# Second attention of a two-layer gated cross-attention kernel: the order of VectorE's work in a step

## The chip, the cores and the metric

The kernel runs on one core of a Trainium2 chip. The metric is the time of one execution on the device in microseconds, median of several runs. Times within a profile are microseconds from the first instruction of the core.

## The reference, cut to what matters

Sixty-four sequences of 128 tokens with 128 features go through two layers, each a gated cross-attention on a context of 77 tokens and a gated feed-forward part. The first feed-forward is a mixture of 16 experts, the second a matrix in FP8 rounding. The change lies in the third pass of the kernel, which finishes the first feed-forward (it gathers the experts' results), and does the second layer:

```
x = x + tanh(g_ffn[0]) * L0_ffn(_layernorm(x))            # its gather and sum are in the third pass
x = x + tanh(g_xattn[1]) * L1_xattn(_layernorm(x), ctx)   # 16 heads of 8, softmax over 77 keys
x = x + tanh(g_ffn[1]) * L1_ffn(_layernorm(x))            # quantize, 128 x 128 matmul, bias
_layernorm(x) = (x - mean(x)) / sqrt(var(x) + 1e-5)
```

## The kernel before, in words

All engines run their own program and meet at semaphores. The kernel has three passes: the first attention and routing (to about 480 us), the experts (to about 700 us), and the second layer, `step_c`. This last pass is a software pipeline: step t works on item t - lag for each operation, with 64 items and 81 steps; `t.at(lag)` gives the item or None where the pipeline fills or drains. The steps are written out one by one. Within a step each engine executes its operations in the order written; a wait at one of them holds everything behind it on that engine. `wait_edge` is a wait that is only emitted for steps below 18 and from 64 on; for the steps between, the order of the others implies it.

The operations that the text speaks of, by line:

- VectorE: L1073 and L1095 add the two gathered expert results to the residual (lag 1). L1078 and L1156 prepare the rounding. L1083 normalises the residual for the attention (`xn3`, lag 2); it needs GpSimd's reciprocal root L637 of the step before. L1065 takes the maxima of the scores in two halves (`largest`, lag 5). L1090 normalises for the last feed-forward (`xb4`, lag 9). L1100 adds the attention's result (lag 8); before it stands a wait for the key projection KT of this step. L1108 writes the masked keys. L1117 and L1122 take statistics (lags 8 and 1), L1131 and L1136 aggregate them to mean and variance, L1151 adds epsilon to both variances. L1126 is the reciprocal of the denominators (lag 7), L1141 multiplies the numerators by it (`OT1`), L1161 makes the output.
- GpSimd: L603 (a part of the rounding), L607 (adds a bias to the residual), L595 twice (the indirect gathers of this step's item), L615, L620, L622, L626 (rounding), and last L637, the power -0.5 of both variances, which waits for L1151.
- TensorE: the projections and transposes at the front of a step; then, behind a wait for the product L1141 of the step before, the scores (8 matmul records) and their transposed form ST (48 records) in one run; Y1 and KT (2 records each); mxT, the transpose of the maxima (1 record), behind the wait for both maxima; then the values V1, the denominators and the numerators (24 records each, line L1172 with 128*32 tiles).
- ScalarE: its first operation in a step, L656 twice, waits for ST; L744 is the exponential.

`par` picks one of two buffers. The variances and reciprocal roots have two, so that step t reads what step t - 1 wrote.

Of the kernel before, what the change touches and what calls it, by code (L numbers as in the profile page):

```python
# [7 lines left out]
ALU = mybir.AluOpType  # L8
ACT = mybir.ActivationFunctionType
X = mybir.AxisListType.X  # L10
P = 128
# [41 lines left out]
def wait_free(engine, sem, value):  # L53

    if isinstance(value, int) and value <= 0:
        return
    engine.wait_ge(sem, value)  # L57
# [24 lines left out]
def wait_edge(engine, t, sem, value):  # L82


    if t.edge:
        wait_free(engine, sem, value)


def flamingo_two_layers(nc, a, out, xs_dram, ys_dram):
# [37 lines left out]
    with ctx:  # L127
# [3 lines left out]
        def sem(name):  # L131
            return ctx.enter_context(nc.semaphore(name))
# [49 lines left out]
        PS = ctx.enter_context(nc.psum_tensor("PS", [P, 8, 512], F32))  # L182
# [82 lines left out]
        rd1 = cc(P)  # L265
        OT1 = cc(P)
# [32 lines left out]
        s = {n: sem(n) for n in names}  # L299
# [477 lines left out]
        def _(dve):  # L777
            V = nc.vector
# [8 lines left out]
            def res(b):  # L787
                return XR[:, bass.ds(b, 1), :].rearrange("q o d -> q (o d)")
# [269 lines left out]
            def step_c(t):  # L1058

                def largest(i):  # L1060

                    if (b := t.at(5)) is not None:
                        dve.wait_ge(s["S1_mm"], b + 1)
                        wait_edge(dve, t, s["mxT_mm"], b)
                        V.tensor_reduce(mx1[:, 2 * i * KEYS:2 * (i + 1) * KEYS].rearrange("q (g k) -> q g k", g=2)[:, :, 0:GH],  # L1065
                                        PS[:, 2 * i:2 * i + 2, 0:GH * J].rearrange("q g (h j) -> q g h j", j=J), X,
                                        ALU.max).then_inc(s["mx1_made"], 1)
# [6 lines left out]
                if (b := t.at(11)) is not None:  # L1074
                    p = t.par(11)
                    dve.wait_ge(s["z4_made"], b + 1)
                    wait_free(dve, s["q4_made"], b - 1)
                    V.tensor_scalar(c4[p].bitcast(I32), z4[t.ring(11, 4)].bitcast(I32), EXP_BITS, None,  # L1078
                                    ALU.bitwise_and).then_inc(s["m4_made"], 1)
                if (b := t.at(2)) is not None:  # L1080
                    dve.wait_ge(s["rsc_made"], b + 1)
                    wait_free(dve, s["xT3_mm"], b - 1)
                    V.tensor_scalar(xn3[t.par(2)], res(b), mvc[t.par(1)][:, 0:1], rsc[t.par(1)][:, 0:1], ALU.subtract,  # L1083
                                    ALU.mult).then_inc(s["xn3_made"], 1)
                largest(0)
                largest(1)
                if (b := t.at(9)) is not None:
                    wait_edge(dve, t, s["rsc_made"], b + 8)
                    wait_free(dve, s["z4_made"], b - 1)
# [28 lines left out]
                if (b := t.at(1)) is not None:  # L1118
# [1 line left out]
                    wait_edge(dve, t, s["agg3"], b)  # L1120
                    apart(dve)
                    V.bn_stats(st3, res(b)).then_inc(s["stats3"], 1)  # L1122
                if (b := t.at(7)) is not None:
                    dve.wait_ge(s["den_mm"], b + 1)
                    wait_free(dve, s["OT1_made"], b)
                    V.reciprocal(rd1, PS[:, 1, 0:P]).then_inc(s["rd1_made"], 1)  # L1126
                if (b := t.at(1)) is not None:
                    dve.wait_ge(s["stats3"], b + 1)
                    wait_free(dve, s["xn3_made"], b - 1)
# [2 lines left out]
                if (b := t.at(8)) is not None:  # L1132
# [1 line left out]
                    wait_free(dve, s["xb4_made"], b - 1)  # L1134
                    apart(dve)
                    V.bn_aggr(mvc[t.par(0)][:, 2:4], st4).then_inc(s["agg4"], 1)  # L1136
                if (b := t.at(7)) is not None:
                    dve.wait_ge(s["num_mm"], b + 1)
                    wait_free(dve, s["rd1_made"], b + 1)
                    wait_edge(dve, t, s["Y1_mm"], b)  # L1140
                    V.tensor_tensor(OT1, PS[:, 3, 0:P], rd1, ALU.mult).then_inc(s["OT1_made"], 1)  # L1141

                one, two = t.at(1), t.at(8)
                if one is not None or two is not None:
                    cols = slice(0 if one is not None else 1, 2 if two is not None else 1)
                    if one is not None:
                        dve.wait_ge(s["agg3"], one + 1)
                    if two is not None:
                        dve.wait_ge(s["agg4"], two + 1)
                    wait_edge(dve, t, s["rsc_made"], t.value - 2)  # L1150
                    V.tensor_tensor(vc[t.par(0)][:, cols], mvc[t.par(0)].rearrange("q (l c) -> q l c", c=2)[:, cols, 1],  # L1151
                                    epsc[:, cols], ALU.add).then_inc(s["varc_made"], 1)
                if (b := t.at(11)) is not None:
                    p = t.par(11)
                    dve.wait_ge(s["m4_made"], b + 1)
                    V.tensor_scalar(c4[p], c4[p], FP8_LEAST, FP8_ROUND, ALU.max, ALU.mult).then_inc(s["c4_made"], 1)  # L1156
# [6 lines left out]
            for span in c_spans():  # L1163
                run_steps(dve, NB, *span, step_c, TURN, LEADC)
# [288 lines left out]
```

## Time and profile before

| | |
|---|---|
| median of 3 runs | 1174.06 us (1169.97 to 1175.59) |
| the profiled execution's own time | 1175.44 us |
| its span | 1173.7 us |
| mean granted TensorE clock | 0.957 |
| busy: TensorE, its weight loads, VectorE, ScalarE, GpSimd | 88%, 72%, 70%, 50%, 55% |
| VectorE: L1065 | 128 times, mean 791 ns |
| VectorE: L1126 | 64 times, mean 954 ns |
| GpSimd: L595 (this pass) | 128 times, mean 1005 ns |

"PE" is TensorE's matmul row, "DVE" VectorE, "ACT" ScalarE, "POOL" GpSimd. In a timeline consecutive instructions of one line and kind are merged into one row (xcount), and the brackets give the idle time before the row and what released it. The granted clock is given as a share of 2.4 GHz.

### The profile page before, as it was taken

How to read it: one execution, taken by the hardware profiler on the slowest of the kernel's cores; microseconds unless marked ns; L12 is line 12 of the kernel's file. 1: busy time of each engine (PE TensorE's matmuls, PEld its weight loads, DVE VectorE, ACT ScalarE, POOL GpSimd, SP SyncE). 2: the span in 40 equal slices, each digit the busy share in tenths (PEclk: the TensorE clock that was granted, in tenths of full speed). 3: DMA queues.
4: the chain of work that ended last, by engine and by line, in shares of the span. 5: the costliest groups of instructions: out<-in, count | busy, mean ns of one | idle time of the engine just before them, and what ended most of it. 6: DMA issues, size and time to landing. Idle time of an engine off the chain costs nothing. (4 is left out here: it accounts for less than half of the span.)

```text
span 1173.7 us, 40437 instructions
## 1 busy us (share of the span) xinstructions
PE 1038.0 (88%) x13498; PEld 847.5 (72%) x13498; DVE 821.1 (70%) x2572; ACT 586.3 (50%) x1415; POOL 648.8 (55%) x1155
## 2 busy tenths in 40 slices
PE   4999999987999995699859996899999999998893
PEld 4788887865777774488758984677777777776672
DVE  1777777776777775655525555778888888887784
ACT  2666666653566662244425552345545545454464
POOL 2333333323777677567640005477777777777756
PEclk9999999997999997699979996999999999999997
DMA  3422113221443300244333331111111111111101
GB/s 74 88 49 46 38 45 75 72 68 45 106 105 89 90 19 29 84 137 145 107 92 112 109 91 48 32 30 37 44 40 43 44 40 43 43 41 41 39 24 31
DMA packets 106902, 74.39 MB, mean 63 GB/s; under 512 B 21360, under 2 KB 98288, under 8 KB 106736
## 3 DMA queue, kind: packets, MB, share of 16 engines
q1 hardware_dynamic: 98544, 55.40, 18.0%
q0 software_dynamic: 8192, 16.79, 4.7%
q8 instruction: 102, 1.67, 0.6%
q14 instruction: 64, 0.52, 0.2%
HBM read 38.60 MB, written 33.55 MB: 61 GB/s over the span
## 5 line engine op out<-in xcount | busy, mean ns | idle before, releaser
L656 ACT ACTIVATE arena<-PS 77x512 f32<-77x512 f32 (+4 forms) x736 | 304.9, 441 | 454.9 <-PE PS L1172 265.5
L1172 PE MATMUL PS<-arena 128*32 128x128 f32 (+5 forms) x9488 | 452.6, 291 | 49.9 <-issue 16.7
L1172 PEld LDWEIGHTS PS<-arena 128*32 128x32 f32 (+4 forms) x9488 | 352.0, 145 | 129.7 <-issue 37.1
L1172 PE MATMUL PS<-w,arena 128*128 x960 | 191.7, 318 | 1.2 <-ACT arena L656 0.4
L518 POOL DMA_INDIRECT moe_rows<-arena x128 | 127.4, 996 | 71.8 <-POOL arena L514 49.5
L533 POOL TENSOR_TENSOR arena<-arena,minus_half 128x2 f32<-128x2 f32 (+1 forms) x70 | 47.5, 679 | 188.3 <-DVE arena L830 166.6
L595 POOL DMA_INDIRECT arena<-moe_results,slot x128 | 128.7, 1005 | 40.7 <-issue 31.6
L1172 PEld LDWEIGHTS PS<-w,arena 128*128 128x128 f32 x960 | 135.5, 195 | 17.0 <-issue 4.5
L637 POOL TENSOR_TENSOR arena<-arena,minus_half 128x2 f32<-128x2 f32 (+1 forms) x71 | 51.1, 720 | 172.7 <-DVE arena L1151 168.9
L1053 DVE TENSOR_TENSOR arena<-PS,b_rows 128x256 f32<-128x256 f32 x160 | 67.8, 424 | 79.0 <-PE PS L1172 65.5
L1172 PEld LDWEIGHTS PS<-arena,wk_wq 128*128 128x128 f32 x512 | 80.6, 198 | 45.6 <-issue 43.0
L1172 PE MATMUL PS<-wo,arena 128*128 128x128 f32 x640 | 100.0, 288 | 2.2 <-ACT arena L656 1.4
L1172 PE MATMUL PS<-arena,wk_wq 128*128 128x154 f32 x512 | 98.3, 317 | 1.5 <-ACT arena L656 0.8
L1065 DVE TENSOR_REDUCE arena<-PS 128x8 f32<-128x616 f32 x128 | 96.0, 791 | 3.3 <-PE PS L1172 3.2
L719 ACT ACTIVATE arena<-PS 128x256 f32<-128x256 f32 x160 | 61.4, 384 | 72.7 <-PE PS L1304 66.9
L1172 PEld LDWEIGHTS PS<-wo,arena 128*128 128x128 f32 x640 | 83.9, 193 | 13.6 <-ACT arena L656 3.4
L744 ACT ACTIVATE arena<-PS 128x1536 f32<-128x1536 f32 x64 | 93.3, 1457 | 0.0
L540 POOL TENSOR_TENSOR arena<-arena 128x616 f32<-128x616 f32 x64 | 78.1, 1220 | 21.6 <-DVE arena L896 21.5
L867 DVE TENSOR_REDUCE arena<-PS 128x8 f32<-128x616 f32 x64 | 51.2, 800 | 54.2 <-PE PS L1172 54.2
L1046 DVE TENSOR_TENSOR arena<-PS,b_rows 128x128 f32<-128x128 f32 x160 | 46.1, 288 | 34.3 <-PE PS L1172 31.3
L1249 PE MATMUL PS<-ident,arena 128*77 128x128 f32 x512 | 68.8, 277 | 1.1 <-ACT arena L656 0.9
L1126 DVE RECIPROCAL arena<-PS 128x128 f32<-128x128 f32 x64 | 61.1, 954 | 12.3 <-PE PS L1172 8.8
(149 smaller groups left out, 1656.5 us busy)
## 6 DMA issues: line engine op xcount, KB each, us to landing
moe_rows<-zeros SPq DMA_DIRECT2D x64, 160.0 KB, 2.5
arena<-moe_rows SPq DMA_DIRECT2D x40, 256.0 KB
moe_results<-arena SPq DMA_DIRECT2D x40, 256.0 KB
residual<-in_x SPq DMA_DIRECT2D x64, 64.0 KB
w<-in_W SPq DMA_DIRECT2D x32, 128.0 KB
arena<-in_ctxC SPq DMA_DIRECT2D x64, 64.0 KB
out<-arena SPq DMA_DIRECT2D x64, 64.0 KB, 1.6
arena<-in_ctxT SPq DMA_DIRECT2D x32, 77.0 KB
```

Of the source, the lines that this page charges most:

```text
L518: g.indirect_dma_start(out=xs_flat[c][:, :], out_offset=bass.IndirectOffsetOnAxis(ap=si[2 * p + k], axis=0), in_=scat[p], in_offset=None). ...
L540: g.tensor_tensor(pv, pv, rd0[t.par(3)].rearrange("q (h o) -> q h o", o=1).to_broadcast([P, H0, J]), ALU.mult).then_inc(s["P0_made"], 1)
L595: g.indirect_dma_start(out=gy[k][p], out_offset=None, in_=ys_flat[c][:, :], in_offset=bass.IndirectOffsetOnAxis(ap=POS[k][:, b:b + 1], axi ...
L656: A.activation(o, i, ACT.Copy).then_inc(s[done], 1)
L719: A.activation(hT[p], PS[:, 4 + p, 0:EH], ACT.Relu).then_inc(s["hT_cp"], 1)
L744: A.activation(PT1[t.par(6)].rearrange("q (g w) -> q g w", g=NG), PS[:, 4:4 + NG, 0:TAIL], ACT.Exp, scale=DH1 ** -0.5).then_inc(s["exp1"], 1)
L867: V.tensor_reduce(mx0.rearrange("q (k h) -> q k h", k=2), sv, X, ALU.max).then_inc(s["mx0_made"], 1)
L1053: V.tensor_tensor(hb[p], PS[:, 2 + p, 0:EH], b1s[:, bass.ds(e, 1), :].rearrange("q o h -> q (o h)"), ALU.add).then_inc(s["h_made"], 1)
L1065: V.tensor_reduce(mx1[:, 2 * i * KEYS:2 * (i + 1) * KEYS].rearrange("q (g k) -> q g k", g=2)[:, :, 0:GH], PS[:, 2 * i:2 * i + 2, 0:GH * J] ...
L1126: V.reciprocal(rd1, PS[:, 1, 0:P]).then_inc(s["rd1_made"], 1)
L1172: return T.matmul(o, l, r, start=start, stop=stop)
L1249: last = T.transpose(PS[0:J, 2 + h // HB0, (h % HB0) * P:(h % HB0 + 1) * P], P0[p][:, h * J:(h + 1) * J], ident[:, :])
```

## The change

In VectorE's `step_c` the two calls of `largest` move ahead of the first normalisation (L1080 to L1084), and the reciprocal and the product move from between the statistics to behind the addition of epsilon. No operation is added or removed.

```diff
+                largest(0)
+                largest(1)
                 if (b := t.at(2)) is not None:
                     dve.wait_ge(s["rsc_made"], b + 1)
                     wait_free(dve, s["xT3_mm"], b - 1)
                     V.tensor_scalar(xn3[t.par(2)], res(b), mvc[t.par(1)][:, 0:1], rsc[t.par(1)][:, 0:1], ALU.subtract,
                                     ALU.mult).then_inc(s["xn3_made"], 1)
-                largest(0)
-                largest(1)
...
                     V.bn_stats(st3, res(b)).then_inc(s["stats3"], 1)
-                if (b := t.at(7)) is not None:
-                    dve.wait_ge(s["den_mm"], b + 1)
-                    wait_free(dve, s["OT1_made"], b)
-                    V.reciprocal(rd1, PS[:, 1, 0:P]).then_inc(s["rd1_made"], 1)
...
                     V.bn_aggr(mvc[t.par(0)][:, 2:4], st4).then_inc(s["agg4"], 1)
-                if (b := t.at(7)) is not None:
-                    dve.wait_ge(s["num_mm"], b + 1)
-                    wait_free(dve, s["rd1_made"], b + 1)
-                    wait_edge(dve, t, s["Y1_mm"], b)
-                    V.tensor_tensor(OT1, PS[:, 3, 0:P], rd1, ALU.mult).then_inc(s["OT1_made"], 1)
...
                                     epsc[:, cols], ALU.add).then_inc(s["varc_made"], 1)
+                if (b := t.at(7)) is not None:
+                    dve.wait_ge(s["den_mm"], b + 1)
+                    wait_free(dve, s["OT1_made"], b)
+                    V.reciprocal(rd1, PS[:, 1, 0:P]).then_inc(s["rd1_made"], 1)
+                if (b := t.at(7)) is not None:
+                    dve.wait_ge(s["num_mm"], b + 1)
+                    wait_free(dve, s["rd1_made"], b + 1)
+                    wait_edge(dve, t, s["Y1_mm"], b)
+                    V.tensor_tensor(OT1, PS[:, 3, 0:P], rd1, ALU.mult).then_inc(s["OT1_made"], 1)
```

## Rows read from the trace of the kernel before

**Rows 1.** Busy time by stretches: us, busy of each engine, clock, DMA share, GB/s

```profile
900.00:1000.00 100.00, 92.68 (x2062) 75.31 (x2065) 85.02 (x270) 51.46 (x135) 78.17 (x135) 1.00 0.15 43
```

**Rows 2.** The reciprocal L1126 counted by stretches: us, VectorE busy (count), clock, DMA

```profile
735.00:770.00 35.00, 4.70 (x5) 1.00 0.11 31
770.00:1060.00 290.00, 41.18 (x43) 1.00 0.15 41
1060.00:1116.00 56.00, 7.42 (x8) 1.00 0.14 39
```

**Rows 3.** Timeline of VectorE, one step: start, us, operation, [idle before]

```profile
904.21 0.15 DVE L1151 TENSOR_TENSOR arena<-arena,eps_columns 128x2 f32<-128x2 f32 x1
...
904.88 0.22 DVE L1078 TENSOR_SCALAR arena<-arena 128x128 int32<-128x128 int32 x1
905.32 0.35 DVE L1083 TENSOR_SCALAR arena<-residual,arena 128x128 f32<-128x128 f32 x1 [0.22 <-POOL arena L637]
905.58 1.50 DVE L1065 TENSOR_REDUCE arena<-PS 128x8 f32<-128x616 f32 x2
...
908.25 0.35 DVE L1100 SCALAR_TENSOR_TENSOR residual<-PS,tanh_gates,residual 128x128 f32<-128x128 f32 x1 [0.65 <-PE PS L1172]
...
909.24 0.28 DVE L1122 BATCH_NORM_STATS2 arena<-residual 128x6 f32<-128x128 f32 x1
909.68 0.96 DVE L1126 RECIPROCAL arena<-PS 128x128 f32<-128x128 f32 x1 [0.16 <-PE PS L1172]
...
910.74 0.29 DVE L1141 TENSOR_TENSOR arena<-PS,arena 128x128 f32<-128x128 f32 x1
```

**Rows 4.** Timeline of TensorE's matmuls, the same step

```profile
904.35 2.14 PE L1172 MATMUL PS<-arena 32*128 32x308 f32 x56 [0.15 <-DVE arena L1141]
...
907.40 1.24 PE L1172 MATMUL PS<-arena 128*32 128x128 f32 x32
908.95 1.34 PE L1172 MATMUL PS<-arena 128*32 128x128 f32 x40 [0.31 <-issue]
```

**Rows 5.** Timeline of GpSimd, the same step

```profile
904.53 0.75 POOL L637 TENSOR_TENSOR arena<-arena,minus_half 128x2 f32<-128x2 f32 x1 [0.72 <-DVE arena L1151]
...
906.16 1.08 POOL L595 DMA_INDIRECT arena<-moe_results,slot  x1 [0.17 <-issue]
...
910.04 0.46 POOL L626 TENSOR_TENSOR arena<-arena 128x128 bf16<-128x128 f32 x1
```

**Rows 6.** Timeline of ScalarE, the same step

```profile
907.51 0.45 ACT L656 ACTIVATE arena<-PS 128x128 bf16<-128x128 bf16 x2 [3.30 <-PE PS L1172]
```

**Rows 7.** Timeline of all engines, a late step without gathers

```profile
1128.80 2.14 PE L1172 MATMUL PS<-arena 32*128 32x308 f32 x56 [0.17 <-DVE arena L1141]
...
1129.67 1.51 DVE L1065 TENSOR_REDUCE arena<-PS 128x8 f32<-128x616 f32 x2 [0.38 <-PE PS L1172]
...
1131.01 0.45 ACT L656 ACTIVATE arena<-PS 128x128 bf16<-128x128 bf16 x2 [2.51 <-PE PS L1172]
...
1131.60 2.17 PE L1172 MATMUL PS<-arena 128*32 128x128 f32 x72
...
1131.60 0.35 DVE L1100 SCALAR_TENSOR_TENSOR residual<-PS,tanh_gates,residual 128x128 f32<-128x128 f32 x1
...
1133.18 0.96 DVE L1126 RECIPROCAL arena<-PS 128x128 f32<-128x128 f32 x1 [0.51 <-PE PS L1172]
```

**Rows 8.** Timeline of all engines, a late step with gathers

```profile
1080.57 2.14 PE L1172 MATMUL PS<-arena 32*128 32x308 f32 x56
...
1081.93 1.08 POOL L595 DMA_INDIRECT arena<-moe_results,slot  x1 [0.17 <-issue]
...
1083.36 1.00 PE L1172 MATMUL PS<-arena 128*32 128x128 f32 x18
...
1084.65 1.75 PE L1172 MATMUL PS<-arena 128*32 128x128 f32 x54 [0.29 <-issue]
...
1084.74 0.45 ACT L656 ACTIVATE arena<-PS 128x128 bf16<-128x128 bf16 x2 [3.86 <-remote]
```

## The prediction

> **What bounds the kernel now.** I read the table of 40 slices first: the change touches only the last of three passes, slices 25 to 40. The busy time by stretches then shows that pass uniform, TensorE at 93%, VectorE at 85%, GpSimd at 78%, the granted clock 1.00, which is 2.4 GHz [rows 1]. No engine is full, so the price of a step lies in a ring of waits between engines. The reciprocal L1126 stands once in a step; counted by stretches it gives 43 steps of 6.74 us from 770 to 1060, five of 7.0 ahead of them and eight of 7.0 behind, then the drain [rows 2]. The chain that ended last covers only the drain, so I took one step from the timelines, engine by engine, zero being the moment at which TensorE issues the scores (904.35).
>
> TensorE's issue is released by the product L1141 of the step before [rows 4]. VectorE [rows 3]: L1151 follows at 904.21, L1083 starts at 905.32, both maxima run from 905.58, L1100 waits 0.65 for TensorE and starts at 908.25, L1126 starts at 909.68 and is released by TensorE, the product L1141 starts at 910.74. The ring is: scores issued (0.00), TensorE's work up to the denominators (5.33 = 909.68 - 904.35), reciprocal and product up to 911.03, 0.05 to the next issue: 6.73 us.
>
> TensorE [rows 4] issues 56 matmuls (scores, then their transposes) from 0.00 on, the last at 2.14 - 0.27 = 1.87, Y1, KT and mxT (5 records) from 2.1 to 2.8, and then 72 (values, denominators, numerators) of which 32 go out before a pause and 40 after it, from 4.60. Its records run ahead of its completions: ScalarE's first copy waits for the transposes and starts at 3.16 [rows 6], 1.0 us behind their last record, and L1100 at 3.90.
>
> The steps after the last gather show what this is [rows 7]. There the 72 run in one piece (2.17), ScalarE starts 2.21 after the issue, L1100 at 2.80, the reciprocal at 4.38 (against 3.16, 3.90 and 5.33). So completions and the pause hang on the two indirect gathers of GpSimd (L595), the first of which starts at 1.81 in the step [rows 5]. In a late step that still has gathers [rows 8] the first starts at 1.36; the copy for the transposes starts only at 4.17; 18 of the 72 go out before the pause and 54 after it. The pause ends 2.72 after the first gather's start there and 2.79 after it in rows 4 and 5. I read this as one mechanism: from at most 0.4 us after the first gather starts (the transposes, natural at 2.21, are already held with a gather from 1.81) TensorE's completions stand, but for some ten that pass in between, until about 2.75 after its start; TensorE goes on issuing until 32 matmuls stand behind the last completed one, then it stops. The count fits at both places: in rows 4 the 32 follow mxT, whose completion is out by then; in rows 8 the 18 with Y1, KT and mxT (5) make 23, and 9 of the transposes are still held.
>
> The Trainium skill (TensorE: Matmul & The Clock Gate, the table of specifications) gives this engine a queue of 64 instructions, the others 8; the 32 matmuls with their 32 weight loads agree. By that rule what counts is how much TensorE still has to issue when the hold begins, so the rule speaks against this change; without it the pause would be the same wherever the gather falls, which is a rival below.
>
> **The change part by part.** (a) L1083 goes behind the maxima. It stands 0.26 (905.58 - 905.32) in front of them and waits 0.22 for GpSimd's L637. The scores are complete 0.87 after their issue (1129.67 - 1128.80, a maximum waiting for them) [rows 7], L1078 ends at 905.10, so the first maximum can start at 905.24 in place of 905.58: up to 0.34 earlier. L1083 itself then starts near 907.0 without a wait; its readers on TensorE come at the next step's front, 3 us later. Nothing else on VectorE before L1100 moves. What the 0.34 is worth is bounded by zero (the maxima were released before the held completions) and 0.34.
>
> (b) L1131, L1136 and L1151 go ahead of L1126. It takes the two aggregates out from between reciprocal (ends at 910.64) and product (starts at 910.74); the product then waits for the reciprocal alone, by my estimate 0.03 less of the 0.10. In front of the reciprocal they make a chain of waits: L1122 starts 0.99 behind L1100, and I put L1151 0.60 behind L1122 (0.28 statistics, 0.12 to 0.15 for each small operation, 0.05 to 0.1 per wait). So L1151 starts 1.6 behind L1100, the reciprocal not before 1.7 behind it. With L1100 where it is (908.25) that is 909.95, 0.27 later than now. Bounds: 0 (L1100 earlier) and 0.35.
>
> (c) The addition L1151 feeds GpSimd's power L637, and behind this stand, on the same engine, L603, L607 and both gathers. From L1151 (904.21) to the first gather (906.16) it is 1.95 [rows 3, 5]. GpSimd is ready before: L626 ends at 910.50 and it then waits 0.72 for L1151. Moved, the gather starts 1.6 + 1.95 = 3.55 behind L1100. The next scores are issued at least 1.7 + 1.37 = 3.07 behind L1100 (1.40 now from reciprocal to issue, less 0.03). So **the first gather falls at most 0.5 us behind the issue of the scores, in place of 1.81**, whatever else moves.
>
> **What follows for TensorE.** The hold begins at 0.5 + 0.4 = 0.9 at the latest, when the 8 matmuls of the scores are just complete and none of the 48 transposes. With ten passing in between, TensorE can issue 8 + 10 + 32 = 50 of its 56 until 0.5 + 2.75 = 3.25. The last 6 (0.03 each) go out at 3.4, in place of 1.87. From there it is the undisturbed order of rows 7: L1100 0.93 later (2.80 - 1.87), at 4.3 to 4.4; the denominators 2.51 later (4.38 - 1.87), at 5.9; the reciprocal behind L1151, at 4.35 + 1.7 = 6.05; the next issue 1.37 on, 7.4. If some more completions pass, or if the gather falls at 0.2, the last of the 56 go out at 3.2 and the step is 7.2. I take 7.3: +0.6 against 6.7. If the hold also catches the completion of the scores, the maxima move to some 1.7, still ahead of the pause's end, so this adds nothing.
>
> Steps [rows 2]: the 43 in the middle are 6.7 and go to 7.3; the five ahead of them go from 7.0 to 7.3; the eight of 1060 to 1116, with more waits and the transposes held to 4.17 already [rows 8], I leave; the drain has no gathers and changes by tenths. Sum: 43 x 0.6 + 5 x 0.3 = 25.8 + 1.5 = +27 us, and one more for the late steps. The profiled execution took 1175.44 us, 1.7 more than its span, and is 1.4 above the median of 1174.06; the sum is one of differences and goes onto the median: **1202 us**. Its own range, 0.35 to 0.8 a step in the middle: 1189 to 1211.
>
> **Rivals.** R1, faster: the hold hurts only what was waiting when it came. With gathers at 0.5 and 1.9 it is over when values and denominators are due, and no pause comes. L1100 then starts when VectorE is free for it, at 3.90 - 0.65 = 3.25, the reciprocal at 4.95, the step is 3.25 + 1.7 + 1.37 = 6.3: 48 x -0.4 = -19, 1155 us. For it: without gathers the reciprocal starts at 4.38. Against: in both places shown the pause comes 2.2 to 2.8 behind the gather's start whatever TensorE has in hand. Chance 0.16.
> R2, slower by little: the pause costs what it costs now wherever it falls, and L1100 stays at 3.9. Then the three small operations hold up the reciprocal by 0.27 less 0.03: 48 x 0.24 = +12, 1186 us. For it: the two pauses differ in their place and hardly in their length. Against: the copy for the transposes is held 1.0 in one and 2.0 in the other. Chance 0.15.
> R3, no change: the pause as now, the earlier maxima bring L1100 forward by 0.3 and hide (b). 1174 us, chance 0.09. It has the price of R2 against it, since L1100 starts on a held completion and not on the maxima.
> The forecast has 0.60.
>
> **Chances.** 0.5% is 5.9 us, about what a measurement of this kernel can tell from no change. Slower: the forecast and R2, 0.75; same: R3 and the weak edge of R2 and R1, 0.10; faster 0.15. The range reaches from part of the faster case to the upper end of the forecast: 1166 to 1213.
>
> **What would show it.** First gather within 0.5 us behind the 56 (now 1.81); the run of 56 itself broken, some 16 of them behind a pause; the 72 in one piece; ScalarE's first copy at 3.6 to 3.8; L1151 ahead of L1126 and the latter released by VectorE's own order; a step of 7.2 to 7.4; L1141's end to the next issue unchanged. Wrong if the 56 go out in one piece with the gather inside them, if L1100 starts before 3.5, or if the late steps grow as much as the middle ones.

## The result, and the profile after

The changed kernel takes 1192.78 us (median of 4 runs, 1191.66 to 1194.08); the kernel before takes 1173.48 (4 runs, 1169.97 to 1175.59). The ratio is 1.0162, 95% interval 1.0149 to 1.0175: slower by 19 us. The forecast was 1202, with 1166 to 1213 as its range: sign right, size too large by half. Spans are 1192.3 and 1173.7 us; by the starts of the product L1141 in both traces they are made of +0.9 in the first eight steps, +18.5 in the forty behind them (0.46 a step) and -0.7 in the late ones. The granted clock is as before (0.958 and 0.957, and 1.00 in this pass).

First the busy time of each engine in the stretch of [rows 1]; the columns are us, then PE, PE's weight loads, DVE, ACT and POOL with their counts, clock, DMA share, GB/s.

```profile
900.00:1000.00 100.00, 88.21 (x1953) 74.07 (x1949) 94.66 (x253) 48.00 (x126) 73.95 (x127) 1.00 0.14 40
```

VectorE went from 85.02 to 94.66 us busy in 100, with fewer instructions (253 against 270); all others fell. So VectorE's instructions got longer, and VectorE is the engine that ran full. Its timeline in one step (start, us, operation, count, and [idle before <- releaser] where it waited), the counterpart of [rows 3]:

```profile
905.50 0.29 DVE L1152 TENSOR_TENSOR arena<-PS,arena 128x128 f32<-128x128 f32 x1
905.71 0.48 DVE L1156 TENSOR_SCALAR arena<-arena 128x128 f32<-128x128 f32 x1
...
906.72 1.51 DVE L1065 TENSOR_REDUCE arena<-PS 128x8 f32<-128x616 f32 x2
908.14 1.00 DVE L1085 TENSOR_SCALAR arena<-residual,arena 128x128 f32<-128x128 f32 x1
908.43 0.78 DVE L1090 TENSOR_SCALAR arena<-residual,arena 128x128 bf16<-128x128 f32 x1
909.12 0.53 DVE L1095 SCALAR_TENSOR_TENSOR residual<-arena,gate_w 128x128 f32<-128x128 f32 x1
909.58 0.34 DVE L1100 SCALAR_TENSOR_TENSOR residual<-PS,tanh_gates,residual 128x128 f32<-128x128 f32 x1
...
910.57 0.27 DVE L1122 BATCH_NORM_STATS2 arena<-residual 128x6 f32<-128x128 f32 x1
910.97 0.18 DVE L1127 BATCH_NORM_AGGREGATE arena<-arena 128x2 f32<-128x6 f32 x1
911.10 0.18 DVE L1132 BATCH_NORM_AGGREGATE arena<-arena 128x2 f32<-128x6 f32 x1
911.38 0.16 DVE L1142 TENSOR_TENSOR arena<-arena,eps_columns 128x2 f32<-128x2 f32 x1
911.49 0.96 DVE L1147 RECIPROCAL arena<-PS 128x128 f32<-128x128 f32 x1
912.55 0.29 DVE L1152 TENSOR_TENSOR arena<-PS,arena 128x128 f32<-128x128 f32 x1
```

(L1085 is L1083 of before, L1127 and L1132 the aggregates, L1142 the addition of epsilon, L1147 the reciprocal, L1152 the product.) In this step no row has a bracket: the 0.65 before L1100 and the 0.16 before the reciprocal are gone, and VectorE waits for nobody (over all middle steps its wait before L1100 is 0.06 on average, 0.59 before). The step, product to product, is 7.05. L1085 takes 1.00 where it took 0.35 [rows 3]. GpSimd and TensorE in the same step, answering to [rows 5] and [rows 4]:

```profile
905.66 0.44 POOL L607 TENSOR_TENSOR residual<-residual,bo 128x128 f32<-128x128 f32 x1
906.28 1.06 POOL L595 DMA_INDIRECT arena<-moe_results,slot  x1 [0.17 <-issue]
907.64 0.95 POOL L595 DMA_INDIRECT arena<-moe_results,slot  x1 [0.30 <-issue]
908.62 0.43 POOL L615 TENSOR_TENSOR arena<-arena,ffn_bias 128x128 bf16<-128x128 bf16 x1
```

```profile
905.85 2.16 PE L1172 MATMUL PS<-arena 32*128 32x308 f32 x52 [0.51 <-DVE arena L1152]
908.22 0.50 PE L1172 MATMUL PS<-arena 32*128 32x128 f32 x4 [0.21 <-issue]
...
909.47 2.17 PE L1172 MATMUL PS<-arena 128*32 128x128 f32 x72
```

The first gather comes 0.43 behind the scores, the run of 56 is broken, the 72 are whole, as forecast. But the break is 4 matmuls behind a pause of 0.21, not some 16. ScalarE's first copy:

```profile
909.24 0.45 ACT L656 ACTIVATE arena<-PS 128x128 bf16<-128x128 bf16 x2 [3.65 <-PE PS L1172]
```

It starts 3.39 behind the scores' issue (3.16 before [rows 6]; 3.6 to 3.8 was forecast).

### The profile page after: what moved, and what is told of

It is laid out like the page before. It is cut to its first block and busy times, and to the rows that moved or that the text cites. A ratio compares the mean times of both kernels' runs of the same rounds, so it can differ in the third digit from the quotient of the medians.

```text
span 1192.3 us, 40437 instructions
## 1 busy us (share of the span) xinstructions
PE 1039.1 (87%) x13498; PEld 857.3 (72%) x13498; DVE 879.3 (74%) x2572; ACT 587.1 (49%) x1415; POOL 650.0 (55%) x1155
## 5 line engine op out<-in xcount | busy, mean ns | idle before, releaser
L1172 PE MATMUL PS<-arena 128*32 128x128 f32 (+5 forms) x9488 | 462.0, 292 | 70.1 <-DVE arena L1152 31.7
L1172 PEld LDWEIGHTS PS<-arena 128*32 128x32 f32 (+4 forms) x9488 | 364.0, 144 | 145.6 <-DVE arena L1152 42.7
L518 POOL DMA_INDIRECT moe_rows<-arena x128 | 127.5, 996 | 71.7 <-POOL arena L514 50.3
L637 POOL TENSOR_TENSOR arena<-arena,minus_half 128x2 f32<-128x2 f32 (+1 forms) x71 | 48.9, 688 | 189.1 <-DVE arena L1142 185.1
L867 DVE TENSOR_REDUCE arena<-PS 128x8 f32<-128x616 f32 x64 | 51.2, 799 | 54.6 <-PE PS L1172 54.6
L1172 PE MATMUL PS<-wv,arena 128*77 128x512 f32 x128 | 67.1, 607 | 0.0
```

What stands on the lines that cost most here:

```text
L518: g.indirect_dma_start(out=xs_flat[c][:, :], out_offset=bass.IndirectOffsetOnAxis(ap=si[2 * p + k], axis=0), in_=scat[p], in_offset=None). ...
L637: g.tensor_tensor(rsc[t.par(0)][:, cols], vc[t.par(0)][:, cols], mhalf[:, cols], ALU.pow).then_inc(s["rsc_made"], 1)
L867: V.tensor_reduce(mx0.rearrange("q (k h) -> q k h", k=2), sv, X, ALU.max).then_inc(s["mx0_made"], 1)
L1172: return T.matmul(o, l, r, start=start, stop=stop)
```

## The experiments

The eleven ran on three chips. On each of them the kernel before takes 1136 to 1137 us, not 1174, so I take the two kernels above to have run on yet another, which I call the first chip; the record does not number it, so this is inferred and not shown. The difference turned out to be strong evidence, and ratios to the kernel before on the same chip are compared, not times. In every trace I cut one of VectorE's steps, near 905 us, into four pieces (the medians over the steps from 770 to 1060 us lie within 0.05 of each entry), each from start to start: product to first maximum, first maximum to L1100, L1100 to reciprocal, reciprocal to product. "First chip" is that of the result; each other line a trace of its experiment.

| kernel | to maximum | to L1100 | to reciprocal | to product | step |
|---|---|---|---|---|---|
| before, first chip | 1.58 | 2.67 | 1.43 | 1.06 | 6.74 |
| after, first chip | 1.22 | 2.86 | 1.91 | 1.06 | 7.05 |
| e5 before | 1.69 | 1.93 | 1.47 | 1.06 | 6.15 |
| e6 after | 1.21 | 2.89 | 1.91 | 1.06 | 7.07 |
| e1 maxima first alone | 1.60 | 2.19 | 1.31 | 1.07 | 6.17 |
| e2 variances ahead alone | 1.47 | 2.58 | 1.90 | 1.06 | 7.01 |
| e3 both gathers later | 1.66 | 2.20 | 1.91 | 1.06 | 6.83 |
| e4 second gather later | 1.22 | 2.34 | 1.91 | 1.06 | 6.53 |
| e7 after, plain loads | 1.61 | 2.19 | 1.92 | 1.06 | 6.78 |
| e8 aggregates alone ahead | 1.57 | 1.94 | 1.62 | 1.07 | 6.20 |
| e9 before, plain loads | 1.55 | 1.99 | 1.40 | 1.06 | 6.00 |
| e10 e1, statistics early | 1.57 | 2.58 | 0.98 | 1.05 | 6.18 |

**e1 and e2: each half alone.** e1 leaves out the second half of the change, e2 the first.

```diff
 # e1, against the kernel before
+                largest(0)
+                largest(1)
                 if (b := t.at(2)) is not None:      # L1083, xn3
...
-                largest(0)
-                largest(1)
```

> The first part of the change alone: both maxima ahead of the first normalisation, reciprocal and product where they were. Theory (hold by place): the additions of epsilon stay behind the product, so the first gather stays 1.8 us behind the issue of the scores, its hold still ends 2.75 us later and the 72 matmuls still break after about 32; the maxima are 0.34 earlier and worth at most 0.05 a step: 1171 to 1174 us. Rival (the maxima count): TensorE's transpose of the maxima goes out 0.3 earlier and the denominators follow it, 0.2 to 0.3 a step: 1160 to 1165 us.

Measured: 1134.63 us, ratio 0.9977 (95% interval 0.9967 to 0.9987, as in the brackets behind all ratios): the earlier maxima are worth 3 us where completions are free. On the first chip this kernel was not run.

> The second part alone: both aggregates and the addition of epsilon ahead of the reciprocal, the first normalisation still ahead of the maxima. Theory (hold by place): it carries the whole loss; first gather within 0.5 us behind the issue of the scores, the run of 56 broken after about 50, the 72 whole, step 7.1 to 7.2 us, 1190 to 1194 us. Rival (the loss comes from the operations that now run beside the second gather: the normalisation took 1.00 us there in place of 0.35): with the normalisation back in front of the maxima it is short again and less than half of the loss is left, 1175 to 1183 us.

Measured: 1175.65, ratio 1.0343 (1.0326 to 1.0361). Nearly all the loss is in the second half. It is 38 us, where the theory had 16 to 20 over a before of 1174 and its rival at most 9. Its trace held the surprise. TensorE's completions are free here: the first copy starts 2.2 behind the scores' issue with a gather beside it, and both long runs of matmuls are whole. By the theory of the prediction nothing but 0.2 a step should have been lost; it is 0.86. In its trace VectorE has no wait, and L1090 and L1095, beside the second gather and what follows it, are long:

```profile
903.23 0.34 DVE L1083 TENSOR_SCALAR arena<-residual,arena 128x128 f32<-128x128 f32 x1
...
904.90 0.77 DVE L1090 TENSOR_SCALAR arena<-residual,arena 128x128 bf16<-128x128 f32 x1
905.58 0.55 DVE L1095 SCALAR_TENSOR_TENSOR residual<-arena,gate_w 128x128 f32<-128x128 f32 x1
```

```profile
902.79 1.06 POOL L595 DMA_INDIRECT arena<-moe_results,slot  x1 [0.17 <-issue]
904.15 0.95 POOL L595 DMA_INDIRECT arena<-moe_results,slot  x1 [0.30 <-issue]
905.13 0.43 POOL L615 TENSOR_TENSOR arena<-arena,ffn_bias 128x128 bf16<-128x128 bf16 x1
```

**e3 and e4: the gathers moved back on GpSimd.** In the changed kernel, both gathers (e3) or the second alone (e4) go behind L622 (`q4`).

```diff
 # e4; e3 moves both
-                    gather(b, t.par(0), t.chunk)
+                    gather(b, t.par(0), t.chunk, (0,))
...
                     g.tensor_tensor(q4, t4, c4[p], ALU.subtract).then_inc(s["q4_made"], 1)
+                if (b := t.at(0)) is not None:
+                    gather(b, t.par(0), t.chunk, (1,))
```

> The changed kernel with both gathers moved on GpSimd behind the second rounding operation (the one that makes q4), so that they start some 1.3 us later, at about 1.8 us behind the scores as in the kernel before. Theory (hold by place): the 56 go out whole again, the 72 are broken after about 32, the denominators are complete at 5.3, and what is left is the reciprocal behind the two aggregates and the addition: step 6.9 to 7.0, 1182 to 1187 us. Rival (the place does not matter, only the order on VectorE): 1191 to 1195 us.

Measured: 1167.47, ratio 1.0276 (1.0258 to 1.0295): 30 us above before, where 8 to 13 were expected.

> The changed kernel with its first gather in place and the second one moved behind the second rounding operation, at some 3.0 us instead of 1.85. One step of the changed kernel's profile happened to have them so (0.48 and 2.93): there the 56 and the 72 both went out whole and the step took 6.39. Theory (hold by place, and each gather alone holds only until some 1.3 us behind its start): every step like that one, 6.3 to 6.5, 1148 to 1160 us. Rival (two gathers cost the same hold together or apart): the pause moves but its sum stays, 1185 to 1195 us.

Measured: 1159.65, ratio 1.0206 (1.0189 to 1.0223). The number lies in the range of the theory by luck: that range was below a before of 1174, and this is 22 us above before. Taking the second gather away from L1085 to L1095 gives back almost half of the loss. TensorE's held completions cannot be the reason, as on these chips they are not held in the changed kernel either (e6). VectorE and GpSimd of e4, one step:

```profile
907.12 0.34 DVE L1088 TENSOR_SCALAR arena<-residual,arena 128x128 f32<-128x128 f32 x1
907.37 0.48 DVE L1093 TENSOR_SCALAR arena<-residual,arena 128x128 bf16<-128x128 f32 x1
```

```profile
906.75 0.46 POOL L620 TENSOR_TENSOR arena<-arena 128x128 f32<-128x128 f32 x1
907.29 0.48 POOL L622 TENSOR_TENSOR arena<-arena 128x128 f32<-128x128 f32 x1
907.99 0.97 POOL L595 DMA_INDIRECT arena<-moe_results,slot  x1 [0.22 <-DVE arena L1093]
```

L1088 (the normalisation, L1085 in the change) is back at 0.34. L1093 is held by L622 and ends 0.08 behind it (907.85 and 907.77). In e3 L607, L613, L618 and L620 of GpSimd stand in one row at the front of the step, and there VectorE's L1162 and L1074 take 0.53 and 0.54 in place of 0.28 and 0.34. So it is not gathers alone that lengthen VectorE's operations.

A second theory came from this, and from here on it stood against the prediction's: the step is a ring of VectorE's own work, lengthened by GpSimd's and by the small operations ahead of the reciprocal.

**e5 and e6: the two kernels themselves on such a chip.**

> The kernel before, unchanged, for a trace from the chip of the other runs. If it takes some 1137 us as on the chip of the first four experiments, TensorE's completions should run free there: the first copy for the transposes 2.2 to 2.6 us behind the product, a step of 6.2 to 6.3, and L1083, L1090 and L1095 at 0.35 each, since the gathers start at 2.0 and 3.4. If it takes 1173, the rows are those of the first trace (copy at 3.2, step 6.7).

Measured: 1135.99 (one run; 12 runs of the same kernel beside it: 1136.04).

> The changed kernel on the chip of the experiments. VectorE theory (the step is a ring of VectorE's own work: L1085, L1090 and L1095 stretched beside the gathers, then 1.9 us from L1100 to the reciprocal): the same step as on the first chip, 7.05 to 7.15, whatever TensorE's completions do, so 1175 to 1185 us. Hold theory (the prediction's: TensorE's held completions set L1100): on a chip where they are not held, no more than the 0.27 of the small operations, about 1150.

Measured: 1179.92, ratio 1.0386 (1.0367 to 1.0406), step 7.07: the VectorE theory's number. VectorE of e6, then of e5:

```profile
901.06 1.51 DVE L1065 TENSOR_REDUCE arena<-PS 128x8 f32<-128x616 f32 x2
902.49 1.01 DVE L1085 TENSOR_SCALAR arena<-residual,arena 128x128 f32<-128x128 f32 x1
902.77 0.79 DVE L1090 TENSOR_SCALAR arena<-residual,arena 128x128 bf16<-128x128 f32 x1
903.49 0.54 DVE L1095 SCALAR_TENSOR_TENSOR residual<-arena,gate_w 128x128 f32<-128x128 f32 x1
903.95 0.34 DVE L1100 SCALAR_TENSOR_TENSOR residual<-PS,tanh_gates,residual 128x128 f32<-128x128 f32 x1
...
904.93 0.27 DVE L1122 BATCH_NORM_STATS2 arena<-residual 128x6 f32<-128x128 f32 x1
...
905.86 0.96 DVE L1147 RECIPROCAL arena<-PS 128x128 f32<-128x128 f32 x1
```

```profile
902.95 0.34 DVE L1090 TENSOR_SCALAR arena<-residual,arena 128x128 bf16<-128x128 f32 x1
...
903.46 0.35 DVE L1100 SCALAR_TENSOR_TENSOR residual<-PS,tanh_gates,residual 128x128 f32<-128x128 f32 x1
...
904.45 0.28 DVE L1122 BATCH_NORM_STATS2 arena<-residual 128x6 f32<-128x128 f32 x1
904.93 0.96 DVE L1126 RECIPROCAL arena<-PS 128x128 f32<-128x128 f32 x1 [0.20 <-PE PS L1172]
```

TensorE and ScalarE of e6: the run of 56 is whole, and the copy starts 2.21 behind its start although the first gather fell 0.42 behind it, as on the first chip.

```profile
900.19 2.14 PE L1172 MATMUL PS<-arena 32*128 32x308 f32 x56 [1.45 <-DVE arena L1152]
```

```profile
902.40 0.45 ACT L656 ACTIVATE arena<-PS 128x128 bf16<-128x128 bf16 x2 [3.63 <-PE PS L1172]
```

GpSimd of e6 shows why L1085 takes 1.01:

```profile
902.00 0.96 POOL L595 DMA_INDIRECT arena<-moe_results,slot  x1 [0.30 <-issue]
902.97 0.44 POOL L615 TENSOR_TENSOR arena<-arena,ffn_bias 128x128 bf16<-128x128 bf16 x1
```

L1085 starts inside the second gather, L615 follows the gather within 0.01, and L1085 ends 0.09 behind L615's end (903.50 and 903.41), L1090 0.06 behind that. Beside the first gather L1073 and L1078 keep their 0.34 and 0.22. The Trainium skill (SBUF — State Buffer, the section on the two separate sides) says that VectorE's operations in a two-port mode, or with two inputs in SBUF against a GpSimd operation that reads SBUF, and GpSimd's operations exclude each other at a shared pair of ports, the loser waiting for the whole instruction. By that rule L1095, with two inputs, waits for L620, L1085 and L1090 wait if they run in a two-port mode, and the maxima, which read PSUM, do not; the durations agree (1.01 against 0.35; the maxima 1.51 in both places).

The traces do not show the wait for the whole instruction everywhere, and there the measurement decides. In the kernel before, L1073 (two inputs) and L1078 (one, 0.22 [rows 3]) stand beside GpSimd's power L637 of 0.75, which runs from 904.53 [rows 5]:

```profile
904.62 0.34 DVE L1073 SCALAR_TENSOR_TENSOR arena<-arena,gate_w,residual 128x128 f32<-128x128 f32 x1
```

Both keep their lengths there, and take 0.54 (L1073, its counterpart in e3) and 0.47 to 0.48 (L1078 beside L607, in three steps of e5) beside operations of 128x128. And within a gather the place counts, not the operation: in e2 L1083, the same operation as L1085, starts 0.44 into the first gather, is done 0.28 before its end, and takes 0.34. In e1 (VectorE, then GpSimd) L1085 starts 0.68 into the first gather, ends 0.03 behind it and takes 0.41, since GpSimd then pauses for 0.30:

```profile
902.19 0.41 DVE L1085 TENSOR_SCALAR arena<-residual,arena 128x128 f32<-128x128 f32 x1
```

```profile
901.51 1.06 POOL L595 DMA_INDIRECT arena<-moe_results,slot  x1 [0.17 <-issue]
902.88 0.99 POOL L595 DMA_INDIRECT arena<-moe_results,slot  x1 [0.30 <-issue]
```

In e6 it starts 0.49 into the second, 0.47 before its end, and L615 follows without a pause. So such an operation is caught only if it is still running near the gather's end, and it is let go at the end unless GpSimd's next operation follows at once. This also answers L1073, which starts 0.04 into the first gather and is long done.

**e7 and e9: no indirect DMA.** Plain loads of fixed rows on SP's queue take the gathers' place, in the kernel after and before; the lookup is left out.

```diff
-                    gather(b, t.par(0), t.chunk)              # GpSimd
+                    sp.dma_start(gy[k][p], ys_flat[0][bass.ds(b * N, N), :]).then_inc(s[f"gy_made{p}"], 16)
```

> The changed kernel without indirect DMA: both gathers are replaced by plain loads of fixed rows on the SP queue, so the lookup is left out. VectorE theory: L1085, L1090 and L1095 go back to 0.35 each, L1100 starts 0.65 earlier, the reciprocal still 1.9 behind it: a step of 6.4, that is 33 us less than the changed kernel on this chip. Rival (the stretching costs nothing, since the maxima and TensorE set L1100): within 5 us of the changed kernel where completions run free.

Measured: 1168.38, ratio 1.0282 (1.0262 to 1.0301). From first maximum to L1100 it gives back 0.70 (2.89 to 2.19), as expected. But only 12 us came back, not 33. Some 6.6 were lost ahead of the steps: the first reciprocal of the pass starts at 731.7, in e6 at 725.1. The rest is at the front of the step: with its gathers gone GpSimd goes straight on to L615 and the rounding, and these now stand beside VectorE's front, where the counterparts of L1161 and L1073 take 0.53 and 0.54 (1.21 to 1.61). The stretching moved; it did not go.

> The kernel before without indirect DMA (plain loads of fixed rows on the SP queue, so the lookup is left out). It tells what the gathers cost the kernel before. If this chip is like the first (before at some 1173): without gathers no completion is held, so the step falls from 6.7 to 6.2 or less and the time by 25 us or more. If it is like the second (before at some 1137, completions free): GpSimd is free 2.4 us earlier, L626 delivers its rows earlier and the scores go out at once, 0.3 of the 6.14, but L1161 and its neighbours on VectorE then run beside L615 to L626 and are stretched as without gathers in the changed kernel: between 1120 and 1140.

Measured: 1130.18, ratio 0.9948 (0.9928 to 0.9968). The kernel is 6 us faster without its gathers, although the first reciprocal of the pass starts 6.1 later than in e5 (732.1 and 726.0); so on a chip that holds nothing the gathers cost the steps of the kernel before about 12 us. The stretching that I expected at its front did not show (L1161's counterpart 0.28). Whether 25 us would come back on the first chip was not seen.

**e8: how much of it is the small operations?** The two aggregates alone go ahead of the reciprocal; the addition of epsilon stays behind the product, and the gathers with it.

```diff
-                    V.reciprocal(rd1, PS[:, 1, 0:P]).then_inc(s["rd1_made"], 1)
...
                     V.bn_aggr(mvc[t.par(0)][:, 2:4], st4).then_inc(s["agg4"], 1)
+                    V.reciprocal(rd1, PS[:, 1, 0:P]).then_inc(s["rd1_made"], 1)
```

> The kernel before with the two aggregates alone ahead of the reciprocal; the addition of epsilon stays behind the product, so GpSimd and the gathers stand as before. VectorE theory: two small operations with a wait each put the reciprocal some 0.35 us further behind L1122, the gathers keep their distance from the scores and nothing is stretched: +0.35 in 48 steps, 17 us over before where completions run free, about 8 where the denominators are held. If the whole loss of the change is the gathers' place, no difference.

Measured: 1141.71, ratio 1.0047 (1.0035 to 1.0060). L1122 to reciprocal is 0.63, against 0.48 in e5 (of which 0.20 is a wait for TensorE) and 0.93 in e6:

```profile
901.49 0.28 DVE L1122 BATCH_NORM_STATS2 arena<-residual 128x6 f32<-128x128 f32 x1
901.89 0.18 DVE L1127 BATCH_NORM_AGGREGATE arena<-arena 128x2 f32<-128x6 f32 x1
902.02 0.18 DVE L1132 BATCH_NORM_AGGREGATE arena<-arena 128x2 f32<-128x6 f32 x1
902.12 0.96 DVE L1136 RECIPROCAL arena<-PS 128x128 f32<-128x128 f32 x1
```

So the aggregates cost 0.15 there and the addition with its wait another 0.30. Against e1, where nothing is waited for (L1122 to reciprocal 0.32), the three cost 0.61. I had put 17 us; it is 5.7, since I had not counted that 0.20 wait, and since 0.12 comes back at the front, where the scores in e5 are late (1.69 and 1.57).

**e10 and e11: a version that beats both?** e10 is e1 with L1122 moved ahead of L1100; e11 is e1 again, beside it.

> Maxima first (the edit of the first half alone) and L1122, the statistics of the combined block, moved from behind L1117 to a place ahead of L1100, where VectorE waits for K's transpose on a chip that holds completions. There 0.27 of VectorE's work goes into a wait of 0.65: 5 to 10 us below the maxima-first kernel if VectorE sets the step, none if the denominators do. On the second kind of chip VectorE has no wait there: within 3 us of the maxima-first kernel, about 1135.

Measured: 1137.56, ratio 1.0003 (0.9992 to 1.0014), 3 us slower than e11 beside it.

> The first half of the change alone, for comparison with the run before it on one chip. Second kind of chip: 0.998 of before, as measured there. First kind: the maxima end 0.34 earlier but L1100 starts on a held completion, so no change, 1170 to 1176.

Measured: 1134.38, ratio 0.9987 (0.9976 to 0.9998). Moving the statistics shifts 0.3 to 0.4 from one piece of the ring to the other (1.31 to 0.98, 2.19 to 2.58) and gains nothing. The maxima first, alone, is the only version with the real lookup that was faster than the kernel before, by 2 to 3 us in both measurements.

## Why the prediction was right and where it failed

The direction and the signs on GpSimd were right; the mechanism that was to make the price was not what made it. That the time fell in the range is therefore in part luck.

**Right.** The maxima come 0.36 earlier (1.22 against 1.58 behind the product; forecast up to 0.34). The first gather falls 0.43 behind the scores (forecast at most 0.5, was 1.81). The addition is ahead of the reciprocal, which is released by VectorE's own order; reciprocal to product stays 1.06. The 56 are broken, the 72 whole. The late steps do not grow on the first chip: there they take 7.3 before (the count in [rows 2] had given 7.0) and 7.1 after. On the chip of e5 and e6 they grow as the middle ones do, most of them from 6.1 to 7.1, which the forecast had named as a sign of being wrong.

**Failed: "Nothing else on VectorE before L1100 moves."** I looked at TensorE's completions when I placed the gathers 1.4 earlier, and never asked what on VectorE would run beside them. L1085, L1090 and L1095 take 1.00, 0.78 and 0.53 in place of 0.35, 0.34 and 0.35; from L1085 to L1100 it is 1.44 where e7, without gathers, has 0.77. That is 0.67 a step. L1083 had run ahead of the maxima, where it cost 0.26; the first half of the change put it just where the second half brought the second gather and L615. The measured halves agree with this, though they come from different chips: first half alone 0.9977, second alone 1.0343, both 1.0386.

**Failed: the hold as the bound.** This is the term that the forecast was added up from. I had TensorE's completions stand until 2.75 behind the first gather and put L1100 at 4.3 to 4.4 behind the issue. They do stand on the first chip (copy at 3.39 against 2.21), but less (20 of the 52 had completed when the queue was full, if 32 stand open as I had it; I had counted 18 of 50), and L1100 starts at 3.73 (909.58 - 905.85), which is where VectorE's own work ends. On the chip of e6 nothing is held and the step is 7.07, the same (some steps are longer on the first chip: 40 reciprocals between 770 and 1060 there, 41 in e6). The three signs of this term missed: the copy at 3.6 to 3.8, the step of 7.2 to 7.4 (7.05), some 16 of the 56 behind the pause (4). So the changed kernel's usual step does not depend on the hold. What depends on it is the step before: 6.74 on the first chip, with 0.65 of waiting before L1100 [rows 3], 6.15 in e5, whose time the kernel before has on all three chips. The loss is therefore 19 us where completions are held and 44 where they are not. The forecast's 0.6 a step came near only because one missing term (0.67 on VectorE) stood in for one too large.

**Mis-sized: the three small operations.** L1142 starts 0.81 behind L1122, not 0.60: the aggregates take 0.18 each ahead of the reciprocal, with a wait at each. L1100 to reciprocal is 1.91, where I had "not before 1.7". Behind the reciprocal the aggregates had run in its shade and cost nothing: reciprocal to product is 1.06 with them and without. This is the mechanism of R2, which gave 1186; the measured time lies between R2 and the forecast, somewhat nearer to R2. Against e5 the terms of a step are: -0.48 at the front, +0.96 from the maxima to L1100 (0.26 L1085's own place, the rest stretching), +0.44 to the reciprocal, 0.92 in all. In the two traces the forty middle steps grow by 36.0 us (0.90 each), the first eight by 2.9 and the later ones by 4.3, 43.2 in all; 43.9 is the difference of the times.

R1 (faster) needed L1100 at 3.25 with VectorE free; VectorE was not. R3 fell with the same row.

**What stays open.** Why completions were held on one chip and not on three others: no experiment ran on the first chip, so that the gathers cause the hold is still the reading of [rows 7], not shown. The two traces of the kernel before (first chip and e5) speak for it in part. Without indirect DMAs they agree: behind the last gather the last three steps take 5.8, 5.8 and 5.7 in both, and the first 33 of the first pass's maxima L867 take 195.0 and 195.9. Beside GpSimd's indirect stores L518 the last 24 of these maxima take 147.9 and 144.8; but the last 64 of these stores, beside the expert pass, take 113.8 and 113.7. Open is also why a gather holds VectorE only towards its end, and the power L637 does not.

## What to carry to other kernels

An operation in the shade of a long instruction is free; put ahead of it, it costs its whole start-to-start time with its waits (here 0.61 for three tiny ones, 0.45 where 0.2 of waiting had stood). When a move shifts the start of work on GpSimd, lay VectorE's timeline over the new place and look at each operation that reads only SBUF: those took 1.5 to 2.9 times as long here, and the loss goes wherever the two overlap, as e7 shows. A bound found in one trace can belong to that chip; ask what would bound the step if it were gone.

## What I had not expected of the hardware

- The same kernel took 1174 us in one place and 1136 to 1137 on three chips, at the same granted clock (0.957 and 0.956). Of the 39 us between the spans (1173.7 and 1134.3) 48 x (6.74 - 6.15) = 28 are in the steps cut above, and 6 fall ahead of the third pass (the experts' last matmul ends at 703.8 and 697.9). In those steps the held copy stands out: ScalarE's copy 3.16 behind the scores on the one, 2.21 on the others.
- A VectorE operation caught by GpSimd ends 0.08 to 0.09 behind the GpSimd operation, whatever its own length, where it has one input in SBUF and goes first: L1085 behind L615, L1093 behind L622, and after the change L1156 (0.48, was 0.22) behind L607 (906.19 and 906.10). With two inputs it is 0.15: L1095 behind L620 (909.65 and 909.50).
